# Handing the walk over the items to SyncE, and moving the sign transposes ahead on TensorE

## The reference

```python
Q, K, V = (x @ W.T per head);  energy = Q @ we.T + be
attn = einsum('hqd,hkd->hqk', Q, K) * 32**-0.5 + energy
attn = attn + where(adj > 0, 0, -inf);  attn = softmax(attn)
hard = (attn == max(attn, -1)) / 8
out = layernorm(x + einsum('hqk,hkd->hqd', hard, V))
```

## Time and profile before

| | |
|---|---|
| median of 3 runs | 1548.78 us (1542.52 to 1553.18) |
| the profiled execution | 1556.98 us, span 1555.2 |
| busy: TensorE matmuls, DVE, ScalarE, POOL | 71%, 65%, 53%, 47% |
| mean granted TensorE clock | 0.898 |
| DMA, mean over the span | 187 GB/s |

### The profile page before, as it was taken

How to read it: one execution, slowest core, us unless ns; L and a number is a source line. 1 busy time by engine, 2 the same in 40 slices (tenths; PEclk the granted TensorE clock), 3 DMA queues, 4 the chain that set the end, 5 groups by cost and what they waited for, 6 DMA issues and landing times.

```text
span 1555.2 us, 46633 instructions
## 1 busy us (share of the span) xinstructions
PE 1096.8 (71%) x12346; PEld 761.7 (49%) x12347; DVE 1016.7 (65%) x3040; ACT 819.2 (53%) x1483; POOL 735.0 (47%) x820
## 2 busy tenths in 40 slices
PE   5878576777777777777766877777666767676671
PEld 3333354555555555555544555555454555454451
DVE  4446377777677767677667667666667666676661
ACT  2332465565555655565555555655565555554551
POOL 0000565666565555565555555454444444444550
PEclk9989799999999999899899898887999988988995
DMA  4642676675656656675666575565656555654550
GB/s 153 219 149 102 194 229 196 179 228 165 222 167 212 210 161 211 202 227 166 209 213 199 168 226 174 193 234 196 195 186 244 204 189 174 227 158 144 163 164 29
DMA packets 87215, 290.88 MB, mean 187 GB/s; under 512 B 14688, under 2 KB 27744, under 8 KB 87200
## 3 DMA queue, kind: packets, MB, share of 16 engines
q0 software_dynamic: 48720, 199.60, 41.5%
q1 hardware_dynamic: 38480, 91.11, 16.8%
HBM read 275.97 MB, written 14.68 MB: 187 GB/s over the span
## 4 chain that ended last, share of the span: by engine, by line
DVE 33%; issue 27%; DVEq 16%; PE 13%; DMA 5%; ACT 2%; another core or an unknown queue 2%; POOL 1%; ACTq 0%; POOLq 0%; SPq 0%
DVE best L758 9%; DVE reached L730 4%; DVE picks L748 4%; DVE hit L736 3%; PE ps_s L925 3%; DMA kv<-kv_table,picks 3%; DVE minus_top L761 3%; DVEq L281 2%; PE ps_s L987 2%; DVE o_all L773 2%; PE ps_s L915 2%; PE ps_s L1006 2%; DMA be_sb<-in_L_gnn_be 1%; DVEq L279 1%
## 5 line engine op out<-in xcount | busy, mean ns | idle before, releaser
L398 POOL DMA_INDIRECT kv<-kv_table,picks x609 | 585.6, 962 | 373.3 <-PE ps_o L1018 169.2
L987 PE MATMUL ps_s<-k_t,q_blk 128*128 128x384 f32 x804 | 381.5, 559 | 31.7 <-ACT masked L478 28.5
L389 POOL TENSOR_TENSOR q_blk<-q_t,minus_same 128x256 f32<-128x256 f32 x202 | 148.0, 733 | 409.7 <-PE ps_s L989 208.3
L489 ACT ACTIVATE hard<-ps_s,minus_top 128x384 bf16<-128x384 f32 x402 | 211.6, 579 | 165.9 <-DVE minus_top L761 149.4
L484 ACT COPY k_t<-ps_s 128x384 f32<-128x384 f32 x404 | 177.7, 482 | 220.4 <-PE ps_s L1006 205.3
L474 ACT ACTIVATE hard_t<-ps_h 128x768 bf16<-128x768 bf16 x200 | 162.2, 811 | 210.0 <-PE ps_h L998 136.7
L1006 PE MATMUL ps_s<-ident_f,kv 128*128 128x128 f32 x1212 | 194.6, 304 | 75.1 <-DMA kv<-kv_table,picks 68.6
L758 DVE TENSOR_REDUCE best<-ps_s 128x1 f32<-128x384 f32 x402 | 205.3, 549 | 45.3 <-PE ps_s L989 23.1
L998 PE MATMUL ps_h<-ident_b,hard 128*128 128x128 bf16 x1200 | 108.8, 231 | 161.4 <-ACT hard L489 136.6
L773 DVE SCALAR_TENSOR_TENSOR o_all<-o_all,keep,ps_o 128x96 f32 x400 | 107.5, 310 | 161.0 <-issue 123.7
L1006 PEld LDWEIGHTS ps_s<-ident_f,kv 128*128 128x128 f32 x1212 | 149.4, 157 | 87.0 <-DMA kv<-kv_table,picks 59.7
(11 more groups left out here) (130 smaller groups left out, 1185.7 us busy)
## 6 DMA issues: line engine op xcount, KB each, us to landing
adj_in<-in_adj SPq DMA_DIRECT2D x128, 512.0 KB
kv_table<-kv_out SPq DMA_DIRECT2D x32, 320.0 KB, 2.4
kv<-kv_table,picks POOLq DMA_INDIRECT x609
x_in<-in_x SPq DMA_DIRECT2D x8, 512.0 KB, 7.6
x_row<-in_x SPq DMA_DIRECT2D x32, 128.0 KB
out<-y_out SPq DMA_DIRECT2D x32, 128.0 KB
w<-in_L_gnn_WQ SPq DMA_DIRECT2D x1, 256.0 KB, 3.0
w<-in_L_gnn_WK SPq DMA_DIRECT2D x1, 256.0 KB, 6.4
```

Of the source, the lines that this page charges most:

```text
L389: pool.tensor_tensor(q_blk[m % 2][:].rearrange("p a (h q) -> p a h q", h=HEADS4), q_t[:, :, bass.ds(at, GQ)].unsqueeze(2).to_broadcast([P, ...
L398: pool.indirect_dma_start(kv[m % RING][:, c, :], None, kv_table, bass.IndirectOffsetOnAxis(ap=picks[m % RING][:, c, 2:3], axis=0)).then_in ...
L489: done = act.activation(hard[m % 2][:, h, :], ps_s[m % 2][h][:, 0:SLOTS], ACT.Sign, bias=minus_top[m % 2][:, h:h + 1], scale=-1.0)
L987: pe.matmul(bank[:, 0:SLOTS], q_blk[m % 2][:, h, :], k_t[m % 2][:, h, :], start=True, stop=False)
```

## The change

SyncE now walks over the items for all engines. For each item it copies one row of a table in HBM (places_of: addresses for DVE's lists, DVE's accumulator, TensorE's values and POOL's queries) into a small tile, plan, by a DMA of 4 x 4 bytes, and for each turn one row of flags: five DMAs a turn, two turns ahead. It does so after the merges of the turn before, and between them issues the adjacency quarters. The engines wait for `planned` once per turn, load four addresses with one instruction and shift them through registers; `walk`, `count_groups` and `plan_turn` go from all their loops. POOL and ScalarE do this at the end of their turns; DVE loads one set between best and minus_top of b = 3 (take_places) and the rest after the last merge (take_plan); TensorE does it before the keys of b = 3. cap and item_slot become tables by address (cap_of, slot_of). TensorE's order within a step becomes `hards_across(m)`, `planes_of(m+4)`, `scores(m+1)` 0 and 1, `keys_across(m+2)`, `values(m)`. Four tiles instead of three get their lists before the loop.

```diff
-FIRST_TILES = 3
+FIRST_TILES = 4
+TURNS = 8
...
+    FIELDS = 4
+    LISTED, RUNNING, VALUES, QUERY = range(FIELDS)
     kv_table = nc.dram_tensor("kv_table", (N, ROW), F32, kind="Internal").ap()
+    places_of = nc.dram_tensor("places_of", (NG * 16, FIELDS), I32, kind="Internal").ap()
+    flags_of = nc.dram_tensor("flags_of", (16, 4), I32, kind="Internal").ap()
...
+        PLANNED = 16 * (RING + 1)
...
+        def run_turns(eng, r, turn):
             with eng.Fori(0, TURNS_OUTER):
-                with eng.If_lt(r["g"], end):
+                with eng.If_ne(r["more"], 0):
                     with eng.Fori(0, TURNS_INNER):
-                        with eng.If_lt(r["g"], end):
+                        with eng.If_ne(r["more"], 0):
                             turn()
 
-        def plan_turn(eng, r):
+        FLAGS = ("fe_on", "fin_on", "te_on", "more")
+        TURN = FLAGS + ("fe", "fin", "te_done", "due", "col", "at_turn")
+
+        def load_places(eng, r, field, names):
+            col = eng.snap(r["col"], min_val=0, max_val=(TURNS - 1) * RING)
+            eng.reg_load([r[k] for k in names], plan[0:1, field, bass.ds(col, RING)])
+
+        def next_turn(eng, r):
             eng.reg_add(r["fin"], r["fin"], r["fin_on"])
-            eng.reg_mov(r["fin_on"], r["fe_on"])
             eng.reg_add(r["fe"], r["fe"], r["fe_on"])
             eng.reg_add(r["te_done"], r["te_done"], r["te_on"])
-            eng.reg_alu(r["te_on"], r["groups"], 2, ALU.arith_shift_right)
-            eng.reg_add(r["limit"], r["te_on"], LEAD)
-            eng.reg_alu(r["limit"], r["limit"], T, ALU.min)
-            eng.reg_alu(r["fe_on"], r["fe"], r["limit"], ALU.is_lt)
-            eng.reg_sub(r["te_on"], r["te_on"], r["te_done"])
-
-        TURN = ("fe", "fe_on", "fin", "fin_on", "te_done", "te_on", "groups", "limit")
+            at = eng.snap(r["at_turn"], min_val=0, max_val=TURNS - 1)
+            eng.reg_load([r[k] for k in FLAGS], turn_flags[0:1, bass.ds(at, 1), :])
+            eng.reg_add(r["due"], r["due"], PLANNED)
+            eng.reg_add(r["at_turn"], r["at_turn"], 1)
+            eng.reg_alu(r["at_turn"], r["at_turn"], TURNS - 1, ALU.bitwise_and)
+            eng.reg_alu(r["col"], r["at_turn"], 2, ALU.logical_shift_left)
+
+        def plan_made(eng, r):
+            eng.wait_ge(planned, r["due"])
+
+        def places(name, first):
+            return [f"{name}{i}" for i in range(first, first + RING)]
+
+        def move_back(eng, r, name, first):
+            for i in range(first, 5):
+                eng.reg_mov(r[f"{name}{i}"], r[f"{name}{i + RING}"])
...
+            def plan_item():
+                sp.reg_add(r["left"], r["left"], -1)
+                sp.reg_add(r["at"], r["at"], 1)
+                with sp.If_lt(r["left"], 1):
+                    sp.reg_add(r["g"], r["g"], 1)
+                    sp.reg_alu(r["at"], r["g"], NG - 1, ALU.bitwise_and)
+                    sp.reg_alu(r["at"], r["at"], 4, ALU.logical_shift_left)
+                    tile = sp.snap(r["g"], min_val=0, max_val=2 * NG - 1) >> 2
+                    lists = (tile & (T - 1)) + 1
+                    sp.wait_ge(counted, lists)
+                    g = sp.snap(r["g"], min_val=0, max_val=2 * NG - 1)
+                    sp.reg_load(r["left"], n_items[P - 1:P, bass.ds(g, 1)])
+                at = sp.snap(r["at"], min_val=0, max_val=NG * 16 - 1)
+                col = sp.snap(r["col"], min_val=0, max_val=TURNS * RING - 1)
+                sp.dma_start(plan[0:1, :, bass.ds(col, 1)], places_of[bass.ds(at, 1), :].unsqueeze(2),
+                             allow_slow_non_contiguous=True).then_inc(planned, 16)
+                sp.reg_add(r["col"], r["col"], 1)
...
+            def plan_turn(first=False):
+                if not first:
+                    plan_flags()
+                sp.reg_alu(r["more"], r["before0"], NG, ALU.is_lt)
+                sp.reg_alu(r["code"], r["more"], 8, ALU.mult)
+                for k, times in (("fe_on", 1), ("fin_on", 2), ("te_on", 4)):
+                    sp.reg_alu(r["limit"], r[k], times, ALU.mult)
+                    sp.reg_add(r["code"], r["code"], r["limit"])
+                code = sp.snap(r["code"], min_val=0, max_val=15)
+                at_turn = sp.snap(r["at_turn"], min_val=0, max_val=TURNS - 1)
+                sp.dma_start(turn_flags[0:1, bass.ds(at_turn, 1), :], flags_of[bass.ds(code, 1), :].unsqueeze(0)
+                             ).then_inc(planned, 16)
+                sp.reg_add(r["at_turn"], r["at_turn"], 1)
+                sp.reg_alu(r["at_turn"], r["at_turn"], TURNS - 1, ALU.bitwise_and)
...
+            def load_part(i):
+                with sp.If_ne(r["fe_on_was"], 0):
+                    with sp.If_lt(r["fe_was"], T - 1):
+                        cast = (sp.snap(r["fe_was"]) & (T - 1)) * QUARTERS + (i + 1)
+                        row = sp.snap(r["fe_was"], min_val=0, max_val=T - 2) * P + P
+                        sp.wait_ge(act_cast, cast)
+                        sp.dma_start(adj_in[:, i * QW:(i + 1) * QW],
+                                     adj[bass.ds(row, P), i * QW:(i + 1) * QW]).then_inc(ld_adj[i], 16)
...
+            def turn():
+                for k in ("fe", "fe_on", "te_on"):
+                    sp.reg_mov(r[f"{k}_was"], r[k])
+                sp.reg_mov(r["te_was"], r["te_done"])
+                load_part(0)
+                sp.wait_ge(planned, r["due"])
+                sp.wait_ge(dve_merge, r["n"])
+                for i in range(RING):
+                    plan_place(i)
+                plan_turn()
+                planned_turn()
+                for i in range(1, QUARTERS):
+                    load_part(i)
+                with sp.If_ne(r["te_on_was"], 0):
+                    row = sp.snap(r["te_was"], min_val=0, max_val=T - 2) * P
+                    rows(sp.snap(r["te_was"]) & (T - 1), row, False)
+                sp.reg_add(r["n"], r["n"], RING)
+
+            run_turns(sp, r, turn)
+            rows(T - 1, (T - 1) * P, True)
...
+                if between is not None:
+                    between()
+                capped = cap_of[:].rearrange("p g i -> p (g i)")[:, bass.ds(at, 1)]
...
+            f = FIRST_TILES
+            word_steps(f, FIN * (f - 1), GPT * (f - 1))
+            ranks(f, FIN * (f - 1), for_item(3)(pe_planes))
+            lists(FIN * (f - 1), GPT * (f - 1), GPT * (f - 1))
+            rank_steps(f, FIN * (f - 1), GPT * (f - 1), None)
+            tops(0, for_item(0), 0)
+
+            def take_places():
+                plan_made(dve, r)
+                load_places(dve, r, LISTED, places("next_listed", 0))
+
+            def take_plan():
+                move_back(dve, r, "listed", 1)
+                move_back(dve, r, "running", 0)
+                for i in range(RING):
+                    dve.reg_mov(r[f"listed{i + 5}"], r[f"next_listed{i}"])
+                load_places(dve, r, RUNNING, places("running", 5))
+                next_turn(dve, r)
+
+            for _ in range(2):
+                take_places()
+                take_plan()
...
-                    if b == 3:
-                        plan_turn(dve, r)
-                    pick(b + 4, for_loop(dve, r, 4), lambda: owners(b + 5, for_loop(dve, r, 5)))
+                    pick(b + 4, for_loop(dve, r, 4), lambda: owners(b + 5, for_loop(dve, r, 5), f"listed{b + 5}"),
+                         f"listed{b + 4}")
                     if b == 1:
...
-                    tops(b + 1, for_loop(dve, r, 1), value_of(dve, bits_of(dve, r["began"], 2), 2))
+                    tops(b + 1, for_loop(dve, r, 1), listed(f"listed{b + 1}"), take_places if b == 3 else None)
                     if b == 0:
                         with front_end_finish(dve, r):
                             dve.wait_ge(pe_pv, for_loop(dve, r, 0)(pe_pv))
                             word_steps(fin() + 1, fin() * FIN, table())
                     if b == 3:
-                        with front_end_finish(dve, r):
+                        with front_end(dve, r):
                             dve.wait_ge(pe_pv, for_loop(dve, r, 0)(pe_pv))
-                            words(fin() * QUARTERS, fin() * FIN)
-                    merge(b, for_loop(dve, r, 0), dve.snap(r["groups"]) & (2 * GPT - 1))
+                            words(tile_of(dve, r, "fe") * QUARTERS, tile_of(dve, r, "fe") * FIN)
+                    merge(b, for_loop(dve, r, 0),
+                          dve.snap(r[f"running{b}"], min_val=0, max_val=(2 * GPT - 1) * HALVES * PARTS * HD))
                     dve.reg_add(r["n"], r["n"], 1)
-
-            run_items(dve, r, 6, turn)
+                take_plan()
+
+            run_turns(dve, r, turn)
...
+            f = FIRST_TILES
+            flags_across(FIN * (f - 1), (xt_copied, 2 * G))
+            word_step(FIN * (f - 1))
+            ranks(f, FIN * (f - 1), for_item(4)(dve_reached))
+            rank_step(FIN * (f - 1), None)
...
+                    hards_across(b, for_loop(pe, r, 0))
```

(51 more changed lines are left out.)

153 lines of the change are left out of this document (100 added, 53 removed).

## The result

Both kernels were run in turn on the same chip. The changed kernel's median is 1697.32 us (1695.96 to 1706.91, 4 runs), the kernel before 1546.87 (1542.52 to 1553.18, 4 runs): a ratio of **1.098**, 95% interval 1.093 to 1.104. The direction was forecast, the size was not: 1697 lies above the range of 1520 to 1690. The profiled execution took 1695.96 us, its span is 1694.2, its mean granted clock 0.868 (before 0.898).

The account below looks back on a forecast made before the run. DVE's own queue, chiefly the walk, was taken to bound the kernel. 1557 + 46 (gaps and second loop) + 24 (clock) + 8 (gathers) = 1635; the execution lying 8 above the median, 1627 us, range 1520 to 1690.

Parts of the forecast that it names:

- signs of being wrong: Hit starting right after the merge, plain turns under 20.3 us, or DVE idling between best and minus_top.
- the new gap cannot be under 2.1: DVE, minus_top to hit: signs and start 1.14, transposes 0.35, sums 0.55, hand-over 0.05 us.
- +0.2 per ordinary gap: DVE, minus_top to hit: wait for TensorE replaces the walk, 2.1 us against 1.9.
- the old gap: DVE, minus_top to hit in the kernel before, walk included: about 1.9 us.
- Where the casts are: ScalarE: 1.15 us casts ahead of two items' signs in F (front-end tile) turns; T (tile-finishing) turns +1.2 us.
- Reading the plan: DVE, end of turn: loads, moves and sums leave 1.1 to 1.85 us uncovered; 1.1 taken.
- A load of four registers: DVE's plan reading: taken at one load's price; at four times, 2.1 us more per turn, 105 us.
- The clock: TensorE's low clock slows transposes and sums in the gap: 18 to 81 us, +24 taken.
- Gathers: TensorE's keys waiting for gathers, now in the second loop: 0 to 68 us, +8 taken.
- SyncE: Five small DMAs a turn, some 5 us, 8 with register work; 9 us left for landing, costed at nothing.
- rival (c): DVE at b=3 waits for a late plan, 3 us in 29 turns: 1714 us, or 1732 with four-fold loads; chance 0.11.
- The possible gain: DVE's gap without the walk: 1.0 us for each of 200 items, 200 us, if nothing is late next.

Follow-up runs that it names:

- experiment 6: Changed kernel, SyncE issuing a turn's five planning DMAs before it waits for the first adjacency cast: 1713.56 us, 1.100 of the kernel before.
- experiment 9: Changed kernel, TensorE waiting for its own signal of the one-hot sums before the scores: 1663.13 us, 1.081 of the kernel before.
- experiment 7: Changed kernel, ScalarE's casts of adjacency quarters 1 and 3 moved behind the signs: 1692.71 us, 1.090 of the kernel before.
- experiment 4: Changed kernel, twenty 64-column filler matmuls per item ahead of TensorE's wait for the signs: 1749.24 us, 1.120 of the kernel before.
- experiment 1: Changed kernel in TensorE's old order (one-hot sums, first score half, sign transposes, second score half): 1526.55 us, 0.982 of the kernel before.
- experiment 5: Changed kernel in TensorE's old order, planning DMAs issued before the wait for the first adjacency cast: 1507.03 us, 0.971 of the kernel before.
- experiment 10: Experiment 5 with TensorE waiting for its own signal of the sign transposes before the second score half: 1436.73 us, 0.933 of the kernel before.
- experiment 11: Kernel before, TensorE waiting for its own signal of the sign transposes before the second score half: 1537.48 us, 0.997.

## Why the prediction was wrong in size

**Held.** The walk left DVE's chain: 161.0 to 15.2. Sums queued behind the transposes make hit wait for TensorE, in 113 of 204 cases instead of 2. SyncE's plan is in time in this kernel (experiment 6). TensorE's wait for the signs was over 1 us in 169 of 200 items. ScalarE's signs started over 0.3 us after minus_top in 88 of 200, behind masks or casts as in the lines above. None of the signs of being wrong appeared: plain turns took 26.0, and no engine waited for the plan.

**The step that failed: "the new gap cannot be under 2.1", and from it "+0.2 per ordinary gap".** The 2.1 was a lower bound and I summed with it as if it were the value. The measured mean is 3.6. By its own terms, over 200 items: minus_top to the transposes' start, forecast 1.14, measured 0.36 + 1.05 + 0.06 = 1.47, since the signs often start late; transposes to sums, forecast 0.35, measured 0.55, since in 56 items the matmuls of the front end's ranks and rank steps stand between the two (0.91 there, 0.41 in the others, where some ran at the low clock); sums to hit, forecast 0.60, measured 1.58, by far the largest miss. In the last piece lie the late signal (0.44 in a hit that waits: 1.14 against the 0.70 of experiment 9), the ranks and rank_steps that DVE can do only after the sums, and the reading of the plan at the boundary. For the old gap I took 1.9 from ordinary items and corrections for the rest; its mean over all was 2.78, so both sides of the subtraction were too small. The mean gap grew by 0.83, not 0.2: 165 us. Of it 0.20 per item came back between hit and best, and 0.05 was lost again behind best.

**The front end's ranks** were left out. They wait for the same sums, 115 us in 54 times now. I let the word steps run inside the 2.1 and did not ask about the ranks; they lie behind it.

**Where the casts are.** I put them in F turns; they lie in the turn ahead, one I mostly called T. T rose by 4.0, not 1.2. By experiment 7 the casts themselves are worth 12 us, which is within its noise.

**Reading the plan** was taken at 1.1 us, with 0.25 of loop 1.35 from the merge's end to hit. Measured:

```profile
1257.09 0.54 DVE L918 SCALAR_TENSOR_TENSOR o_all<-o_all,keep,ps_o 128x96 f32 x2
1259.66 0.32 DVE L878 SCALAR_TENSOR_TENSOR hit<-ps_x,slot_of,slot 128x96 f32<-128x96 f32 x1 [2.03 <-issue]
```

2.03, the upper end of my bounds: 0.7 a turn too little, 34 us in the old order, where 50 hits waited so (105.4 us); in the changed kernel only 27 did, the rest is covered. A load of four registers is not four times as dear: DVE's loads from plan take 0.344 us, that of one register took 0.318.

**The clock** fell more often, as I said. TensorE's score matmuls show it (groups of instructions, before and after):

```profile
L987 PE MATMUL ps_s<-k_t,q_blk 128*128 128x384 f32 x804 | 381.5, 559 | 31.7 <-ACT masked L478 28.5 <-issue 0.7
```

```profile
L1153 PE MATMUL ps_s<-k_t,q_blk 128*128 128x384 f32 x804 | 443.1, 640 | 0.0
```

542 ns is the median in both, so all of the mean's rise is the low level. Items with a score group over 1.4 us went from 30 to 90 of 200. What that cost stays open. The transposes' busy time rose from 108.8 to 120.5 us and the sums' from 120.8 to 131.1; they lie in the gap, so 22 us is my estimate for it there, near the 24 that I took. Comparing items inside a trace does not settle it: the low ones took 7.52 us against 7.32 of the others in the changed kernel, but 7.51 against 7.73 in experiment 4 and 7.56 against 6.97 in experiment 9. The Trainium skill (TensorE: Matmul & The Clock Gate, "What's actually happening") calls the throttled state the default, released by activity; the trace agrees in direction: TensorE's busy share fell from 71% to 66% and its mean clock from 0.898 to 0.868.

**Gathers**, +8: the wrong sign, TensorE's stall for them fell by 56 us, much of which had been hidden.

**SyncE** at nothing was right for this kernel only. I gave the five issues 5 us, 8 with register work. In the changed kernel's trace four of them with the walk between took

```profile
581.07 7.89 SPq L388 DMA_DIRECT2D plan<-places_of  x4
```

and all five 9.6 us. Most of it is the walk: an issue itself (ns, shortest, median, longest) is dearer for 16 bytes in four pieces than for an adjacency quarter of 512 KB, but by 0.34 us only:

```profile
L388 SPq DMA_DIRECT2D plan<-places_of x208: 12/674/1009, 118.1 to 1642.8; - x104
L458 SPq DMA_DIRECT2D adj_in<-in_adj x108: 3/336/361, 188.2 to 1477.4; - x108
```

Between them stand the load of n_items (0.448 us at the median), sums and branches. So SyncE pays for the walk that it took over. In the old order a late plan like that of my rival (c) cost some 1% (experiments 1 and 5). The Trainium skill (DMA: Bandwidth & Descriptors, "Rules for kernel authors") says that small transfers pay mostly overhead; the trace agrees as far as the issue goes, which is no cheaper for 16 bytes. I had put that overhead into the latency, which no view here shows for these DMAs.

**The possible gain** of 200 us from the walk: 28 us as built but in the old order, 45 with the plan first, 103 with the own wait. Each next wait ate the rest.

**Open.** Why the signal is held: that it is late only with matmuls queued behind the group is shown by experiments 9 to 11, by which mechanism is not. The profile models the end of a matmul, so it can't tell whether the work ends late or its signal alone. What the low clock costs on the chain is open too; part of what the own wait gave may be clock, which rose with it (median over the runs 0.869 to 0.881 in experiment 9, 0.912 to 0.927 in 10). The new order with all three repairs (plan first, casts behind, own waits) was not run, nor a turn with a cheaper plan.

## What to carry to other kernels

An engine's queue is in order: before moving a step ahead, list every engine that waits for what is now behind it, the rare work of a turn too, and sum with the measured lateness of the step's input, not with the shortest case. A bound from below is not an estimate. Where another engine waits for a group of matmuls and more are queued behind, try a wait of TensorE on its own signal, one at a time, and only where the waiting engine is on the chain: here it gave 3.9% in one kernel, 1.5% in a second, 0.3% in a third, and another wait added to the first took 2.8 points away.

## What the hardware showed that was not expected

- With others queued behind it, a group's signal reached a waiting engine up to 2.35 us after the group's start (one-hot sums of 0.50 us, changed kernel). The same transposes of 0.50 us released ScalarE after 2.14 us in one item of experiment 5 and after 0.53 in one with an own wait, which stopped TensorE for 0.23.
- One own wait per item removed the late signals of the other groups as well: DVE's "remote" waits went from 62.6 us to none (experiments 5 and 10).
- To issue a DMA of 4 x 4 bytes with strided ends held SyncE's queue for 0.67 us at the median, a flags row of 16 contiguous bytes for 0.64, an adjacency quarter of 512 KB for 0.34.
- Twenty small matmuls per item ahead of TensorE's wait for the signs raised the mean clock by 0.017 only and cost 2% of the time (experiment 4).
